# A 17-stage decoder kernel on one core: weights of five more stages loaded one stage early, tables prepared behind the scales, VectorE's order in the linear attention changed

## The reference

```python
# a0: 16 heads of 8, rotary, a fixed table added to the scores
scores = q @ k.T / sqrt(8) + slopes * rel;  out = softmax(scores) @ v @ Wo.T
# c0, c3: cross attention, keys and values from ctx, a fixed bias table; c3 masks keys
scores = Q @ K.T / sqrt(8) + bias;  out = softmax(scores) @ V @ Wo.T + bo
# a1: linear attention with its own residual and layer norm
qf, kf = elu(x@Wq+bq)+1, elu(k)+1;  num = qf @ cumsum(kf v);  den = qf @ cumsum(kf) + 1e-6
y = x + (num/den) @ Wo + bo;  f = (y-mean(y))/sqrt(var(y)+1e-5)*gamma + beta
# f2: causal attention among the 64 rows of highest router score (here all 64, in router order), then g2
g2: x_ff = silu(h2 @ W1.T) * (h2 @ W2.T) @ W3.T
```

## Time and profile before

| what | value |
|---|---|
| median of 3 runs | 7300.41 us (7296.68 to 7302.1) |
| the profiled execution, its own time | 7294.51 us |
| its span in the trace | 7292.4 us |
| mean granted TensorE clock | 0.961 of full |
| busy: PE, DVE, ACT, POOL | 6507.4, 5360.5, 4055.2, 2820.5 us |

### The profile page before, as it was taken

One profiled execution on the slowest core, in us unless ns is written; L12 is line 12 of the kernel. 1 busy time (PEld: TensorE's weight loads), 2 busy tenths in 40 slices (PEclk: granted clock), 3 DMA queues, 4 the chain that ended last, 5 costly groups with the idle time before them and its releaser, 6 DMA issues. The chain is left out here.

```text
span 7292.4 us, 189527 instructions
## 1 busy us (share of the span) xinstructions
PE 6507.4 (89%) x74836; PEld 3973.7 (54%) x74836; DVE 5360.5 (74%) x8933; ACT 4055.2 (56%) x6024; POOL 2820.5 (39%) x1680
## 2 busy tenths in 40 slices
PE   7989987887697989989999779989899999989998
PEld 5767665444442333333333356666576767667676
DVE  7877576665556999999999856677577777768544
ACT  3556343665446777777777745455344444456433
POOL 3321175332214888888888601165021212211000
PEclk9999978999888999999999989999999999999999
DMA  1000000000001222222222100000000000000000
GB/s 29 0 21 13 3 11 8 3 3 2 14 2 52 76 73 75 75 80 77 76 75 76 51 12 13 9 31 3 12 2 2 2 2 2 2 15 14 2 0 23
DMA packets 115881, 190.04 MB, mean 26 GB/s; under 512 B 38661, under 2 KB 74746, under 8 KB 114970
## 3 DMA queue, kind: packets, MB, share of 16 engines
q1 hardware_dynamic: 112218, 183.47, 7.9%
q10 hardware_dynamic: 3264, 0.54, 0.1%
HBM read 173.87 MB, written 7.98 MB: 25 GB/s over the span
## 5 line engine op out<-in xcount | busy, mean ns | idle before, releaser
L2600 POOL TENSOR_TENSOR m_dBx<-m_dtx,m_Bs 128x1024 f32<-128x1024 f32 x515 | 1165.8, 2283 | 227.3 <-DVE m_hs L2965 185.2
L2965 DVE TENSOR_TENSOR_SCAN m_hs<-m_ps_dA,m_dBx 128x512 f32<-128x512 f32 x1030 | 1200.5, 1207 | 56.4 <-POOL m_dBx L2600 55.8
L2719 PE MATMUL m_ps_y<-m_yc,ident 128*128 128x512 f32 x2060 | 1021.6, 619 | 0.0
L2824 ACT ACTIVATE m_ps_dA<-m_dt,m_A 128x504 f32<-128x504 f32 x1030 | 682.0, 678 | 427.1 <-DVE m_hs L2965 424.4
L2096 POOL TENSOR_TENSOR a_s<-a_s,a_den 128x1024 f32<-128x1024 f32 x128 | 243.5, 1902 | 1123.9 <-DVE a_den L2142 1123.9
L2976 DVE TENSOR_TENSOR m_yc<-m_hs,m_ps_C 128x1024 f32<-128x1024 f32 x515 | 616.3, 1197 | 1.3 <-PE m_ps_C L2700 1.3
L2719 PEld LDWEIGHTS m_ps_y<-m_yc,ident 128*128 128x128 f32 x2060 | 350.5, 190 | 357.0 <-issue 357.0
L2700 PE MATMUL m_ps_C<-m_parts,m_sel 48*128 48x512 bf16 x516 | 199.8, 387 | 175.7 <-DVE m_yc L2976 175.6
L2700 PEld LDWEIGHTS m_ps_C<-m_parts,m_sel 48*128 48x128 bf16 x516 | 47.7, 92 | 566.9 <-DVE m_yc L2976 421.2
L625 POOL TENSOR_TENSOR c_kbd<-c_kf,c_hmask 128x1024 f32<-128x1024 f32 x66 | 125.0, 1893 | 515.9 <-ACT c_kf L534 492.0
L2140 DVE TENSOR_REDUCE a_den<-a_s 128x16 f32<-128x1024 f32 x128 | 156.0, 1219 | 207.0 <-ACT a_s L2047 207.0
(11 more groups left out here) (748 smaller groups left out, 16025.2 us busy)
## 6 DMA issues: line engine op xcount, KB each, us to landing
m_Bs<-BC_rows SPq DMA_DIRECT2D x258, 512.0 KB, 3.5
c_kvb<-in_ctxT SPq DMA_DIRECT2D x68, 128.0 KB, 2.1
c_kvb<-in_ctxT SPq DMA_DIRECT2D x17, 256.0 KB, 2.7
out_dram<-X SPq DMA_DIRECT2D x1, 4096.0 KB
BC_rows<-m_low SPq DMA_DIRECT2D x33, 64.0 KB, 2.7
part_rows<-m_split SPq DMA_DIRECT2D x33, 48.0 KB, 1.7
m_parts<-part_rows SPq DMA_DIRECT2D x33, 48.0 KB, 1.7
m_piece<-BC_rows SPq DMA_DIRECT2D x33, 32.0 KB, 1.7
```

The lines of the kernel that those rows point to most:

```text
L2600: return nc.gpsimd.tensor_tensor(to, one, other, ALU.mult)
L2719: last = nc.tensor.matmul(ps_y[:, m, :], C.ident[:], of[:, m, :], start=s == 0, stop=s == NS - 1)
L2824: nc.scalar.activation(seqs(ps_dA[:, h % 3, :]), seqs(dt[:, par, m, :]), ACT.Exp, scale=A[:, second, m, s:s + 1]).then_inc(decay, 1)
L2965: nc.vector.tensor_tensor_scan(hs[:, s % HS, m, :], ps_dA[:, (2 * s + m) % 3, :], dBx[:, s % BX, m, :], 0.0, ALU.mult, ALU.add).then_inc(s ...
```

## The change

1. The tiles of a0, c0, f2, c3 (`table_shapes`) and g2 (`gated_shapes`) are made beforehand by `Weights`, and all their loads, the late ones too, are issued a stage or more earlier: a0's by ScalarE during `load_x`, c0's in a0, f2's in c2, g2's and a3's in f2 (both; `follow` now takes several names), c3's in g2. `load_x` is now called from `first_blocks`. `late_loaded` is gone.
2. In a cross attention SP issues the first two pieces of ctx before the following stage's weights.
3. In c0 and c3 VectorE runs `prepare_table` before `diagonal_values` of the first unit; in a0 it stays behind the second queries.
4. In a1 `row_sums`, `add_rows` and `new_sums` become one `joint` behind `diagonal_values`; the centring moves from in front of the residual to behind it, the new statistics lag one unit more (w-4) and are written to `C.MV` in every slot by a `tensor_tensor` max of a tile with itself.

```diff
 def load_following(C, sp):
-    if C.following is not None:
-        C.ahead[C.following].start(sp)
+    for name in C.following:
+        C.ahead[name].start(sp)
...
+        @block.scalar
+        def _(act):
+            load_following(C, act)
...
+def table_shapes(W):
+    shapes = dict(wq=[P, D], wk=[P, D], wv=[P, D], wo=[P, D], hmask=[P, HR])
+    if "tril" in W:
+        shapes.update(tril=[P, S], g1=[P, 1], wr=[P, D])
+    else:
+        shapes.update(table=[P, NH, S])
...
+def table_loads(t, W):
+    return [(tensor[:], bc(W["bo"], [P, D]) if n == "bo" else W["mask" if n == "keepi" else n]) for n, tensor in t.items()]
...
         @block.sync
         def _(sp):
-            for to, of in loads:
-                sp.dma_start(to[:], of).then_inc(loaded, 16)
-
-            load_following(C, sp)
-
             def load(par, at):
                 sp.dma_start(kvb[:, par, :], kT_dram[:, at]).then_inc(kv_loaded[par], 16)
             if cross:
                 for par in range(2):
                     load(par, slice(par * UC, par * UC + UC))
-            for to, of in late:
-                sp.dma_start(to[:], of).then_inc(late_loaded, 16)
+            load_following(C, sp)
...
-            pe.wait_ge(late_loaded, n_late)
             scores(0, 0)
...
+            if cross:
+                prepare_table()
             take_keys(0, True)
             take_queries(0, True)
             diagonal_values(0, 0)
             take_keys(1)
             take_queries(1)
-            if not rank:
+            if rope:
                 prepare_table()
...
+            def joint(w, par, centre=True, sums=True, new=True):
+                if centre:
+                    for t in range(UT):
+                        y = row(C.Y, (w - 1) * UT + t)
+                        nc.vector.scalar_tensor_tensor(y, y, mv[:, (1 - par) * UT + t, 0:1], gamma[:], ALU.subtract, ALU.mult)
+                if sums:
+                    for t in range(UT):
+                        nc.vector.bn_stats(st[:, t, :], row(C.Y, w * UT + t))
+                if new:
+                    for t in range(UT):
+                        nc.vector.bn_stats(st2[:, t, :], row(C.X, (w - 2) * UT + t))
                 dve.drain()
+                if sums:
+                    for t in range(UT):
+                        last = nc.vector.bn_aggr(mv[:, par * UT + t, :], st[:, t, :])
+                    last.then_inc(var_ready, 1)
+                if new:
+                    for t in range(UT):
+                        nc.vector.bn_aggr(mv2[:, t, :], st2[:, t, :])
+                if centre:
+                    dve.wait_ge(rs_ready, w)
+                    for t in range(UT):
+                        x = row(C.X, (w - 1) * UT + t)
+                        nc.vector.scalar_tensor_tensor(x, row(C.Y, (w - 1) * UT + t), rs2[:, 1 - par, t:t + 1], x, ALU.mult, ALU.add)
+                if new:
                     dve.drain()
+                    new_rows = C.MV[:, bass.ds((w - 2) * UT, UT), :]
+                    tt(new_rows, mv2[:], mv2[:], ALU.max)
...
+            def slot(w, u, weigh=True, project=True, finish=2):
                 mask(w, u)
                 if weigh:
                     normalise(w - 1)
-                if finish:
-                    add_rows(w - 3, 1 - u)
                 if project:
                     residual(w - 2)
                 diagonal_values(w, u)
                 if project:
-                    row_sums(w - 2, u)
-                if finish:
-                    new_sums(w - 3, i - 1 - (1 - u), 1 - u)
+                    dve.drain()
+                    joint(w - 2, u, finish > 0, True, finish > 1)
...
+            follow(C, "a0")
+            load_x(C, A["x"], A)
+            follow(C, "c0")
+            attn16_table(C, "a0", "rope", a0)
...
+            follow(C, "f2")
             attn64(C, "c2", c2, 1, 1, A["ctxT"])
...
+            follow(C, "g2", "a3")
+            attn16_table(C, "f2", "rank", f2)
+            follow(C, "c3")
+            gated_ffn(C, "g2", g2)
```

More of the change, by code:

```diff
@@ L31, in __init__ @@
         self.nc, self.NG, self.NT = nc, groups, groups * TPG
-        self.ahead, self.following = {}, None
+        self.ahead, self.following = {}, ()
         pad = self.NT + 2 * TPG
@@ L231 @@
 HV = NB * HD
+def table_shapes(W):
[4 more added lines that the diff above has]
+        shapes.update(table=[P, NH, S])
+    if "bo" in W:
+        shapes.update(bq=[P, 1], bk=[P, 1], bv=[P, 1], bo=[P, D])
+    if "cosT" in W:
+        shapes.update(cosT=[P, S], sinT=[P, S])
+    if "mask" in W:
+        shapes.update(keepi=[P, S])
+    return shapes
+def table_loads(t, W):
+    return [(tensor[:], bc(W["bo"], [P, D]) if n == "bo" else W["mask" if n == "keepi" else n]) for n, tensor in t.items()]
 def attn16_table(C, name, mode, W, kT_dram=None):
@@ L242, in attn16_table @@
     with ExitStack() as ctx:
-        sc = Scope(nc, ctx, name)
+        sc = Scope(nc, ctx, name, C.ahead[name])
         sb, ps, sem = sc.sb, sc.ps, sc.sem
@@ L296, in attn16_table @@
         block = ctx.enter_context(nc.Block())
[L297 to L309, removed]
+        n_loaded = 16 * len(C.ahead[name].loads)
         n_prepared = 2
@@ L1211, in add_rows @@
[L1211 to L1220, removed]
@@ L1256, in _ @@
             normalise(n)
-            row_sums(n - 1, 0)
-            add_rows(n - 2, 1)
             dve.drain()
-            new_sums(n - 2, C.NG - 2, 1)
+            joint(n - 1, 0)
             residual(n)
-            row_sums(n, 1)
-            add_rows(n - 1, 0)
             dve.drain()
-            new_sums(n - 1, C.NG - 1, 0)
-            add_rows(n, 1)
+            joint(n, 1)
             dve.drain()
-            new_sums(n, C.NG - 1, 1)
+            joint(n + 1, 0, True, False, True)
+            dve.drain()
+            joint(n + 2, 1, False, False, True)
 class Front:
@@ L1319, with gated_chunks, gated_shapes, gated_loads @@
 PAIR = 2 * TPG
+def gated_chunks(W):
+    F = W["w1"].shape[1]
+    return [(f, min(P, F - f)) for f in range(0, F, P)]
+def gated_shapes(W):
+    F = W["w1"].shape[1]
+    return dict(w1=[P, F], w2=[P, F], w3=[P, len(gated_chunks(W)), D], g=[P, 1])
+def gated_loads(t, W):
+    return [(t[n][:], W[n]) for n in ("w1", "w2", "g")] + [
+        (t["w3"][0:n, c, :], W["w3"][f:f + n, :]) for c, (f, n) in enumerate(gated_chunks(W))]
 def gated_ffn(C, name, W):
@@ L1325, in gated_ffn @@
     F = W["w1"].shape[1]
-    chunks = [(f, min(P, F - f)) for f in range(0, F, P)]
+    chunks = gated_chunks(W)
     NF = len(chunks)
     with ExitStack() as ctx:
-        sc = Scope(nc, ctx, name)
+        sc = Scope(nc, ctx, name, C.ahead[name])
         sb, ps, sem = sc.sb, sc.ps, sc.sem
@@ L1345, in _ @@
         def _(sp):
[L1346 to L1349, removed]
             load_following(C, sp)
-        n_loaded = 16 * (3 + NF)
+        n_loaded = 16 * len(C.ahead[name].loads)
         @block.tensor
@@ L4190, in first_blocks @@
               hmask="hmask", triu="triu", gamma="gamma", beta="beta")
+    a0 = pick(A, "a0_", cosT="cosT", sinT="sinT", table="table0", **qkvo)
+    c0 = pick(A, "c0_", bq="bq", bk="bk", bv="bv", bo="bo", table="table1", **qkvo)
     with ExitStack() as ctx:
@@ L4193, in first_blocks @@
         Weights(C, ctx, "f0", lora_shapes, lora_loads, f0)
[L4194 to L4197, removed]
+        with ExitStack() as tables:
+            Weights(C, tables, "c0", table_shapes, table_loads, c0)
+            Weights(C, tables, "a0", table_shapes, table_loads, a0)
+            follow(C, "a0")
+            load_x(C, A["x"], A)
+            follow(C, "c0")
+            attn16_table(C, "a0", "rope", a0)
+            follow(C, "f0")
+            attn16_table(C, "c0", "ctx", c0, A["ctxT"])
         follow(C, "a1")
@@ L4234, in last_blocks @@
     f3 = pick(A, "f3_", wr="wr", w1="w1", w2="w2", falling="falling")
+    f2 = pick(A, "f2_", g1="g1", wr="wr", tril="tril", **qkvo)
+    g2 = pick(A, "f2_", w1="w1", w2="w2", w3="w3", g="g2")
+    c3 = pick(A, "c3_", bq="bq", bk="bk", bv="bv", bo="bo", table="table3", mask="mask", **qkvo)
     with ExitStack() as last:
         Weights(C, last, "f3", topk_shapes, topk_loads, f3)
+        Weights(C, last, "c3", table_shapes, table_loads, c3)
+        Weights(C, last, "g2", gated_shapes, gated_loads, g2)
+        Weights(C, last, "f2", table_shapes, table_loads, f2)
         with ExitStack() as ctx:
@@ L4247, in last_blocks @@
             Weights(C, ctx, "a3", attn64_shapes, attn64_loads, a3)
[L4248 to L4251, removed]
+            follow(C, "g2", "a3")
+            attn16_table(C, "f2", "rank", f2)
+            follow(C, "c3")
+            gated_ffn(C, "g2", g2)
             follow(C, "f3")
             attn64(C, "a3", a3, 4, 2)
-        follow(C, None)
-        attn16_table(C, "c3", "mask", pick(A, "c3_", bq="bq", bk="bk", bv="bv", bo="bo", table="table3", mask="mask", **qkvo), A["ctxT"])
+        follow(C)
+        attn16_table(C, "c3", "mask", c3, A["ctxT"])
```

41 lines of the change are left out of this document (11 added, 30 removed).

## The result

The changed kernel takes 7322.6 us (median of 8, 7317.5 to 7333.1) beside 7301.5 (median of 8) for the one before: a ratio of 1.0029, 95% interval 1.0019 to 1.0040. It is slower by 21 us, where 41 less were forecast. The profiled execution took 7317.9 (span 7316.1).

What follows compares the result with a forecast made beforehand. Stages chained by barriers, each worth its own last wait, TensorE busiest, VectorE bounding a1's slot; +2.0 - 0.2 - 10.0 - 0.75 - 2.65 - 3.0 - 26.0 = -40.6 from 7300.4 gave 7260 us, range 7246 to 7288.

Steps and rivals of the forecast that it cites:

- a1, -26 forecast: Linear attention loop: slots go from 7.74 to 7.5 us and nearly all clock falls vanish, -26 us.
- VectorE's work per slot stays the same: a1's loop: the new order adds no VectorE work, so fewer drains shorten the slot from 7.74 to 7.5 us.
- Half a copy (0.09 lost): a1's loop: storing statistics every slot instead of every second costs half a 0.17 us copy, 0.09 us a slot.
- a1 gives nothing: Rival for a1: drains were free and the clock behaves as now; sum -14.6, 7286 us, chance 0.12.
- The sign named beforehand: a1's loop: the forecast is wrong if the mean clock stays at 0.85, which alone is 20 us.
- the wait for ScalarE's inverse root: a1: a new VectorE wait for this result, due a slot earlier, would show the forecast wrong; no size given.
- The clock: a1's loop: shorter TensorE waits leave one clock fall of seven, at 3 us; 28 slots take 213 us, -25.7.
- c0 and c3: Cross attention starts: scores come earlier, limited by the values' copy behind the table; -10.0 us in c0, -3.0 in c3.
- f2, g2: Stage starts: f2 gains -0.75 us until GpSimd's mask holds it, g2 gains -2.65 us of weight wait.
- Load and a0: Start of kernel: a0's loads delay x's first chunk, +2.0 us; a0's keys matmul comes earlier, -0.2 us.
- Heads in sum: All terms outside a1, the load and the starts of a0, c0, f2, g2, c3: together -14.6 us.
- more falls in a1: Rival for a1: finer gaps bring the clock down in every pair of slots, +21.4 us; 7307 us, chance 0.04.

Runs made afterwards that it cites:

- experiment 5: Changed kernel with a1's statistics stored by ScalarE from a double buffer instead of VectorE, and 17 drains behind a1 restoring the code's place: 7255.1 us, ratio 0.9936.
- the run with all edits: Changed kernel plus ScalarE's store in a1, code place restored, values' copy inside c0's and c3's table preparation, a0's loads after x's second chunk: 7265.8 us, ratio 0.9940.

## Why the prediction was wrong

- **The step that failed first** is one that was not there. The sum went through the stages that the diff touches and gave the others 0, as if a stage's time hung on its own code alone. It also hangs on where its loop lies in the engine's program. That term measured +35 (three drains take 27 to 30 back in the medians), and makes the sign. Without it the time would have been 7296, still outside the range, because of the next step.
- **a1, -26 forecast, +0.3.** The failed step is "VectorE's work per slot stays the same". It was counted with durations from an order in which the scalings seldom fell beside a two-operand operation of GpSimd. In the new order they fell on them far more often: the loop's VectorE time grew by 19 us, the slot at full clock was 7.63 to 8.46 and not 7.5, and the clock still fell, six times for some 14 us and twice for less, where it had been seven times for 10. "Half a copy (0.09 lost)" was 0.52 + 0.17 us in each slot, the largest single part. The price of a drain itself was right: 0.17 us ahead of each store, 0.2 forecast. The outcome for a1 is that of the rival "a1 gives nothing" (0.12), but by another cause than its "drains were free". The sign named beforehand, a mean clock that stays near 0.85, came; the wait for ScalarE's inverse root did not.
- **The clock.** That with shorter waits the falls would go was possible, but not by this change: in experiment 5's profile they are gone, and the 28 slots took 201 us where 213 was forecast. In the profile of the run with all edits, with the same order and store, four short falls and two longer ones are left, and the slots took 222. The new order was needed for it and not enough.
- **c0 and c3.** What is late next was named rightly (the values' copy). The size was off: the preparation meets GpSimd's product, 1.6 us each, and in c0 the clock had fallen, where the term had it up. c0 gave -7.6 for -10, less than its lower bound of 8.5. c3 gave -2.8 for -3.0, which is in part luck: its first scores came 1.1 us earlier and not 2.7, and the rest came in slots that the forecast left alone.
- **f2, g2.** The forecast instruction came 0.64 and 2.6 us earlier (-0.75 and -2.65). The g2 stage got only 0.9 shorter; what held it then wasn't traced.
- **Load and a0.** +1.2 for +2.0. a0's +1.7 can't be told from its spread: it took 366.6 to 370.1 in all these profiles.
- **Heads in sum:** -12 us measured with a1's old order (interval -18 to -4), where -14.6 was forecast. That part held within the noise. In the profiles the touched stages without a1 give -9.
- **Range and chances.** The only rival on the slower side was "more falls in a1", at 0.04. The slower kernel came by a mechanism that no rival held, and the range ended 35 us below the result.

## What to carry to other kernels

When an edit changes the number of instructions of an engine, count the later loops of that engine against the block edges: by the count that held here, a loop of 257 to 512 instructions fits into two blocks of 256 at some places and not at others, and a few idle instructions in front of it settle it. When a VectorE operation is moved, cost it with what GpSimd does at the new time, not with its old duration. After a change that gives nothing, look for the one small operation that still stands in the rhythm: here it was a store of four numbers per partition, worth 38 us of the total with the new order. And before a stage's time in one profile is called a gain, look where that execution stands among the others: a1 took 255 us in the fastest of one kernel and 280 in the slowest of another, with the same code.

## What the runs showed of the hardware

- A VectorE loop of 302 instructions cost 28 to 30 us in waits when it stood one or three instructions earlier in the program, and nothing in its old place; seven turns moved some five packets each on the instruction queue (40 in all for 6). Shifted on by 196, it cost nothing and the loop of 304 ahead of it 15 us.
- A VectorE operation on 128x4 elements took 0.16 us alone and up to 1.60 beside GpSimd's two-operand operations. A copy was held by them in the same way, and by GpSimd's one-operand clipping as well (0.32 us). The clipping held no scaling in the changed kernel; in the run with a1's old order four scalings beside it took 0.58 to 0.71 us, for a cause that wasn't looked into.
- The mean granted clock of a1's loop was 0.81 to 1.00 for the same matmuls: 0.81 in the changed kernel, 0.89 with ScalarE's store in the old order, 0.92 and 1.00 in two profiles with both. At 1.00 the 28 slots were 16% shorter than before.
